# Third layer: keys and values in the second layer's normalisation, queries by halves of the tokens

## The chip, the cores and the metric

One program on one core of a Trainium2 chip. The metric is the device time of one execution in microseconds (us); the kernel before has a median of 1384.41 us in three runs (1384.3 to 1389.26). The engines are TensorE (PE in the rows, with its weight loads as PEld), VectorE (DVE), ScalarE (ACT), GpSimd (POOL) and SyncE (SP), whose queue issues nearly all transfers (DMAs).

## The reference

Four layers follow each other. The first is a large cross-attention with a multilayer perceptron. The second and fourth are alike: 16 heads of 16, keys over the context and the tokens, a root-mean-square normalisation and a perceptron. The third is the one whose start is changed. Cut to what matters:

```python
# 4 batches x 256 tokens, width 256; ctx is an input of the whole program
def layer3(x, ctx, mask):                    # 32 query heads of 8, 8 key/value heads
    q = x @ Wq + bq                          # (4, 256, 256)
    k = ctx @ Wk + bk                        # (4, 256, 64): depends on ctx alone
    v = ctx @ Wv + bv                        # (4, 256, 64): depends on ctx alone
    scores = einsum(q, k) / sqrt(8) + mask   # each key head serves 4 query heads
    out = softmax(scores) @ v @ Wo + bo
    return layernorm(out + x) * gamma + beta
x = layer3(layer2(ctx, layer1(x, ctx), m0), ctx, mask)
x = layer4(ctx, x, m0)
```

## The kernel before

The 1024 tokens (T) lie in 8 tiles of 128 partitions; `core.x` holds them token-major, `core.cT` holds the context feature-major. The program is a row of stages. Each is one block with one instruction stream for each engine, written by hand, and at its end all engines meet; inside, semaphores order them. No scheduler moves anything: the order in the code is the order on each engine, and a DMA is issued when SP reaches it. A stage also ends only when SP has passed its own waits.

The stages around the change, in order:

- `project_out` of the second layer (stage o1) multiplies the attention's output by its matrix and adds the residual.
- `rms_turn` (stage r1) normalises: VectorE takes the statistics of 8 tiles, GpSimd raises them to -1/2, ScalarE scales tiles 0 to 3 and VectorE tiles 4 to 7 (`normed`, L564 and L597). TensorE turns each half with 8 transposes (L611); ScalarE and VectorE split the result into a high and a low part (L568, L601). Beside it the perceptron's first weights are loaded and split, high parts on ScalarE (L1300), low parts on GpSimd (L1305).
- `mlp` (stage m1) is the perceptron; `next_layer` 2 makes SP load the third layer's `wq`, `wkv` and `bv_row` there (L66 to L71).
- `turn` (stage t2) turns `core.x` into `xT`: 16 transposes (L530), and 4 copies on VectorE (L523).
- `wide_projections` (stage p2) computes keys (group 0 and 1, one per half of the tokens), queries (groups 2 to 5: rows `m` 0 with both halves, then `m` 1 with both) and values (8 tiles). For each group TensorE multiplies, VectorE adds the bias (`q_f`), ScalarE rounds it (`q_hi`), VectorE takes the rest (`q_lo`). SP stores keys and queries to DRAM (`k_stack`, `q_stack`) and reads them back in another layout (`load_keys`, `load_queries`). Query stores go by `m`, for all tokens; half of batch 0's heads need only `m` 0, yet SP has `m` 1's stores ahead of their loading:

```python
stores(1)                      # keys
stores(3)                      # queries, m 0, all tokens
sp.wait_ge(k_stored, 16 * 3)
load_keys(c, sp, k_stack, k_st, 0, first_in)
stores(5)                      # queries, m 1, all tokens
sp.wait_ge(q_stored[0], 16 * 3)
load_queries(c, sp, q_stack, q_st, 0, slice(0, c.NQ // 2), first_in)
sp.wait_ge(mask_in, 16); sp.wait_ge(q_stored[1], 16 * 3); sp.wait_ge(first_in, 16 * 8)
```

- `wide_attention` (stage s2) takes 32 quads (4 heads of one batch). Its SP stream first loads the other half of batch 0's queries, then keys and queries of batches 1 to 3. Its first scores are L1887.

The fourth layer (stages p3, s3 and so on) uses `pair_attention`, as the second does; its rounds end with the copy L2023.

Of the kernel before, what the change touches and what calls it, by code (L numbers as in the profile page):

```python
# [5 lines left out]
P = 128  # L6
B = 4
# [499 lines left out]
def turn(core, name, src, xT):  # L507

    nc, ident = core.nc, core.ident
    with core.stage(name) as st:  # L510
        turned = st.psum("turned", [P, 4, 512])
        tile_turned = st.sem("tile_turned")
        chunks = [(kt, slice(half * 512, (half + 1) * 512)) for half in range(2) for kt in range(KT)]
        with nc.Block() as block:
            @block.gpsimd
            def _(pool):
                core.clear_used(pool)

            @block.vector
            def _(dve):  # L520
                for n, (kt, cols) in enumerate(chunks):
                    dve.wait_ge(tile_turned, n + 1)
                    nc.vector.tensor_copy(xT[:, kt, cols], turned[:, n, :])  # L523

            @block.tensor
            def _(pe):
                for half in range(2):
                    for kt in range(KT):
                        for i in range(4):
                            mm = nc.tensor.transpose(turned[:, KT * half + kt, i * P:(i + 1) * P],  # L530
                                                     src[:, 4 * half + i, kt * P:(kt + 1) * P], ident[:])
                        mm.then_inc(tile_turned, 1)


def rms_turn(core, name, src, ahead, eps, scale):
# [6 lines left out]
    with core.stage(name) as st:  # L542
# [9 lines left out]
        chunks = [(kt, slice(half * 512, (half + 1) * 512)) for half in range(2) for kt in range(KT)]  # L552

        with nc.Block() as block:
            @block.sync
            def _(sp):
                ahead.prepare_sync(sp, z)

            @block.scalar
# [1769 lines left out]
```

## Time and profile before

| what | us |
|---|---|
| median of three runs | 1384.41 |
| profiled execution, its own time | 1390.04 |
| its span | 1388.2 |
| PE busy in the span | 1230.7 (89%) |
| last operation of the second layer's perceptron begins | 969.01 |
| first scores of the third layer begin | 1001.86 |
| o1: SP issues its two loads, the second ends | 896.5 |
| o1: its last operation ends, on VectorE | 906.69 |
| `wq` of the second layer: issue to landing, median of 2 | 5.9 |

The profiled execution is 5.6 us longer than the median, near the slowest of the three runs. Times inside it are read from the span's start; 1.84 us lie around the span. A row of the timeline has start, duration, engine, line, operation, out<-in, shapes and count; in brackets stands how long the engine had been idle and what released it. SPq is the issue of a DMA by SP, not its transfer. A matmul of plain f32 shows as two rows' worth of instructions (x8 for 4 matmuls).

### The profile page before, as it was taken

The page shows a single profiled execution, that of the slowest core. Times are in us where ns is not written, and L with a number is a line of the kernel's source. Part 1 is how long each engine was busy: PE and PEld are TensorE (multiplying, and loading weights), DVE is VectorE, ACT ScalarE, POOL GpSimd, SP SyncE. Part 2 cuts the span into 40 slices and gives each one's busy share as a digit, 9 for nine tenths or more (in the row PEclk, how much of TensorE's full clock was granted, in tenths as well). Part 3 has the DMA queues.
Part 4 walks back from the last instruction along what each step waited for, and adds up shares of the span by engine and source line. Part 5 has one row for each costly group of instructions (what it writes and reads, how often), then busy time and mean ns, then how long its engine had stood idle before and what let it go on. Part 6 is the DMA issues. An engine that isn't in the chain of part 4 may idle for free. (4 is left out here: it accounts for less than half of the span.)

```text
span 1388.2 us, 27413 instructions
## 1 busy us (share of the span) xinstructions
PE 1230.7 (89%) x9144; PEld 1014.5 (73%) x9144; DVE 987.8 (71%) x2229; ACT 722.0 (52%) x1636; POOL 495.6 (36%) x642
## 2 busy tenths in 40 slices
PE   5799999999599999999699699969499977699869
PEld 4699999999499999998588455559277756455558
DVE  6478878787578887888763689465488865689464
ACT  4456655666366666566542177441166632177441
POOL 3654545444374445543150000030199940000030
PEclk9899999999799999999899699979799998699979
DMA  4111111010211111010023874020660014874020
GB/s 151 47 31 32 31 30 30 23 30 1 95 32 32 31 31 29 9 38 0 31 65 71 121 83 56 13 77 1 196 131 3 2 51 83 112 81 55 13 65 31
DMA packets 55406, 70.90 MB, mean 51 GB/s; under 512 B 6696, under 2 KB 47404, under 8 KB 52976
## 3 DMA queue, kind: packets, MB, share of 16 engines
q1 hardware_dynamic: 53704, 65.83, 22.8%
q10 hardware_dynamic: 1600, 3.76, 0.9%
q8 instruction: 57, 0.93, 0.3%
q14 instruction: 45, 0.37, 0.1%
HBM read 46.79 MB, written 8.13 MB: 40 GB/s over the span
## 5 line engine op out<-in xcount | busy, mean ns | idle before, releaser
L945 ACT ACTIVATE a_prob<-a_s_ps,a_negmax 128x257 f32<-128x257 f32 x256 | 119.2, 477 | 92.9 <-DVE a_negmax L1027 92.9
L2033 DVE TENSOR_REDUCE s_mx<-s_s_ps 128x2 f32<-128x1024 f32 x128 | 151.9, 1211 | 17.9 <-PE s_s_ps L2078 17.6
L2018 ACT ACTIVATE s_probT<-s_st_ps 128x512 f32<-128x512 f32 x256 | 132.1, 605 | 58.6 <-PE s_st_ps L2092 56.3
L884 POOL TENSOR_TENSOR x_v_hi<-a_v_sum,x_one 128x512 fp32r<-128x512 f32 x60 | 63.2, 1053 | 248.7 <-DVE a_v_sum L1016 248.7
L1822 POOL TENSOR_SCALAR s_below<-s_masked,s_mx 128x256 f32<-128x256 f32 x256 | 117.8, 480 | 30.5 <-DVE s_mx L1850 29.7
L576 POOL TENSOR_TENSOR rstd<-base,power 128x4 f32<-128x4 f32 x4 | 4.0, 1009 | 335.6 <-DVE base L593 335.6
L1042 DVE TENSOR_TENSOR a_pT_lo<-a_t_ps,a_pT_hi 128x512 fp32r<-128x512 f32 x128 | 88.3, 690 | 37.9 <-ACT a_pT_hi L958 36.2
L1027 DVE TENSOR_REDUCE a_negmax<-a_s_ps 128x2 f32<-128x514 f32 x128 | 87.0, 689 | 35.6 <-PE a_s_ps L1088 35.3
L958 ACT ACTIVATE a_pT_hi<-a_t_ps 128x512 fp32r<-128x512 f32 x128 | 76.7, 600 | 59.5 <-PE a_t_ps L1142 56.1
L1850 DVE CUSTOM_DVE_ANT_0 s_masked<-s_s_ps,l_mask 128x256 f32<-128x256 f32 x256 | 90.7, 421 | 16.6 <-PE s_s_ps L1887 16.6
L1835 ACT ACTIVATE s_probT<-s_st_ps 128x512 f32<-128x512 f32 x128 | 69.9, 596 | 29.1 <-PE s_st_ps L1897 29.0
L1086 PE MATMUL a_s_ps<-x_k_hi,x_q_hi 128*128 128x258 f32 x256 | 75.0, 293 | 10.8 <-ACT a_prob L945 5.5
L2078 PE MATMUL s_s_ps<-l_k_st,l_q_st 49*128 49x512 f32 x192 | 68.0, 543 | 15.9 <-PEq L1531 9.5
L1086 PE MATMUL a_o_ps<-a_pT_hi,x_v_hi 128*128 128x256 f32 x256 | 81.1, 317 | 0.0
L1142 PE MATMUL a_t_ps<-ident,a_prob 128*128 128x128 f32 x512 | 78.2, 275 | 3.0 <-ACT a_prob L953 2.0
L2092 PE MATMUL s_st_ps<-l_q_st,l_k_st 50*128 50x256 f32 x384 | 70.4, 339 | 11.0 <-DMA l_q_st<-s_mxT 11.0
L961 ACT ACTIVATE a_oT_hi<-a_o_ps,a_hc 128x256 fp32r<-128x256 f32 x128 | 60.8, 475 | 36.9 <-PE a_o_ps L1088 29.6
L886 POOL TENSOR_TENSOR x_v_lo<-a_v_sum,x_v_hi 128x512 fp32r<-128x512 f32 x60 | 77.3, 1289 | 4.7
L1086 PE MATMUL a_g_ps<-x_wv_hi,c_hi 128*128 128x256 f32 x240 | 70.3, 293 | 7.8 <-POOL x_wv_lo L867 7.8
L2092 PEld LDWEIGHTS s_st_ps<-l_q_st,l_k_st 50*128 50x128 f32 x384 | 48.5, 204 | 34.3 <-DMA l_q_st<-s_mxT 12.8
L1088 PE MATMUL a_s_ps<-x_k_hi,x_q_lo 128*128 128x258 f32 x256 | 72.9, 285 | 0.0
L1087 PE MATMUL a_s_ps<-x_k_lo,x_q_hi 128*128 128x258 f32 x256 | 72.9, 285 | 0.0
(289 smaller groups left out, 4069.0 us busy)
## 6 DMA issues: line engine op xcount, KB each, us to landing
a_wo_raw<-L_xattn_wo SPq DMA_DIRECT2D x16, 256.0 KB, 3.2
x_wqk_raw<-L_xattn_wq SPq DMA_DIRECT2D x31, 128.0 KB, 2.3
x_wqk_raw<-L_xattn_wk SPq DMA_DIRECT2D x31, 128.0 KB, 2.3
x_wv_raw<-L_xattn_wv SPq DMA_DIRECT2D x15, 256.0 KB, 3.0
l_k_st<-k_second SPq DMA_DIRECT2D x12, 256.0 KB, 9.6
l_k_st<-k_stack SPq DMA_DIRECT2D x16, 192.0 KB
l_q_st<-q_stack SPq DMA_DIRECT2D x12, 192.0 KB
x_vbias<-L_xattn_bias_v SPq DMA_DIRECT2D x2, 1024.0 KB, 11.0
```

The costliest lines, as they stand in the source:

```text
L886: nc.gpsimd.tensor_tensor(lo, raw, hi.bitcast(F32), ALU.subtract).then_inc(z.v_split, 1)
L945: nc.scalar.activation(prob[:, n % 2, qt, 0:NK], s_ps[:, n % 2, qt, 0:NK], ACT.Exp, bias=negmax[:, n % 2, qt:qt + 1], accum_out=den[:, n % ...
L958: nc.scalar.activation(pT_hi[:, n % 2], t_ps[:], ACT.Copy).then_inc(z.t_hi, 1)
L1027: nc.vector.tensor_reduce(negmax[:, n % 2], s_ps[:, n % 2, :, 0:NK], AX.X, ALU.max, negate=True).then_inc(z.max_done, 1)
L1042: nc.vector.tensor_tensor(pT_lo[:, n % 2], t_ps[:], pT_hi[:, n % 2].bitcast(F32), ALU.subtract).then_inc(z.t_out, 1)
L1086: nc.tensor.matmul(out, a_hi, b_hi, start=start, stop=False)
L1142: mm = nc.tensor.transpose(t_ps[:, at:at + P], prob[:, n % 2, qt, kt * P:(kt + 1) * P], core.ident[:])
L1822: nc.gpsimd.tensor_scalar(below[:, i % 2, h, qt], masked[:, i % 2, h, qt], -1.0, mx[:, i % 2, h, qt:qt + 1], ALU.mult, ALU.add).then_inc(z ...
L1850: nc.vector.tensor_tensor_reduce(out=masked[:, i % 2, h, qt], in0=s_ps[:, h, qt], in1=mask[:, i // NQ * QT + qt], scale=1.0, scalar=-3.0e3 ...
L2018: nc.scalar.activation(probT[:, third % 2, n // 4, n // 2 % 2, n % 2], st_ps[:, u % 3], ACT.Exp, scale=c.scale).then_inc(z.exp_done, 1)
L2033: nc.vector.tensor_reduce(mx[:, i % 2, qt, a::2], s_ps[:, n % 2], AX.X, ALU.max).then_inc(z.max_done, 1)
L2092: mm = nc.tensor.matmul(st_ps[:, u % 3, j * S:(j + 1) * S], k[:, a, kt * P:(kt + 1) * P], q[:, a], start=True, stop=True)
```

## The change

Three things are done.

1. Keys and values of the third layer are computed in r1, the normalisation of the second layer, by a new class `WideKeys`. SP stores the keys there; the values stay in SBUF (`v_tok`) and GpSimd copies them into `v_st` in p2. For that the third layer's weights are loaded in o1 instead of m1.
2. Stage t2 goes; p2 itself turns `core.x`, the copies shared between VectorE and ScalarE.
3. Queries are computed and stored by halves of the tokens (half 0 holds batches 0 and 1): groups are now (m 0, half 0), (m 1, half 0), (m 0, half 1), (m 1, half 1). SP loads batch 0's keys first, and its queries before the stores of half 1; those are waited for only at batch 2 (`q_late`).

```diff
+class WideKeys:            # k_ps, v_ps: PSUM; f, hi, lo: the keys and their parts, 64 x 1024
+    def keys(self, pe, half):
+        for kt in range(KT):
+            mm = self.nc.tensor.matmul(self.k_ps[0:KW, half], core.wkv[:, kt, 0:KW], core.cT[:, kt, self.cols(half)],
+                                       start=(kt == 0), stop=(kt == KT - 1))
+        mm.then_inc(self.k_done, 1)
+    def values(self, pe):  # 8 tiles x 2 matmuls of 64 columns
...
+    def high(self, act, half):   # two ACTIVATEs: f = k_ps + bias, hi = f
...
+    def low(self, pool, half):   # lo = f - hi
...
+    def store(self, sp):
+        for part, (kept, slots) in enumerate(((self.hi, (0, 2)), (self.lo, (1,)))):
+            sp.wait_ge((self.hi_done, self.lo_done)[part], 2)
+            for n in slots:
+                sp.dma_start(self.front.k_stack[:, n], kept[:].bitcast(F32)).then_inc(self.front.k_stored, 16)
+    def add_bias(self, dve):     # v_tok = v_ps + bias, one 128 x 512 TENSOR_TENSOR
...
 # rms_turn
             def _(act):
+                if keys:
+                    keys.high(act, 0)
                 ahead.prepare_scalar(act, z)
...
+                if keys:
+                    keys.high(act, 1)
                 for n, (kt, cols) in enumerate(chunks):
...
+                if keys:
+                    keys.low(pool, 0)
                 ahead.prepare_pool(pool, z)
+                if keys:
+                    keys.low(pool, 1)
...
+                if keys:
+                    keys.add_bias(dve)
                 for n, (kt, cols) in enumerate(chunks):
...
             def _(pe):
+                if keys:
+                    for half in range(2):
+                        keys.keys(pe, half)
+                    keys.values(pe)
...
 # wide_projections, SP
+                sp.wait_ge(front.k_stored, 3 * 16)
+                load_keys(c, sp, front.k_stack, k_st, 0, z.first_in)
                 sp.dma_start(mask[:], ins["mask_Bx1xSxS2_ff0"].rearrange("b o (t p) k -> p (b o t) k", p=P)
...
+                store(0, z.q_stored0)
+                store(1, z.q_stored1)
+                sp.wait_ge(z.q_stored0, 3 * 16)
+                load_queries(c, sp, front.q_stack, q_st, 0, slice(0, c.NQ // 2), z.first_in)
+                for g in range(2, 4):
+                    store(g, front.q_late)
+                sp.wait_ge(z.mask_in, 16)
+                sp.wait_ge(z.q_stored1, 3 * 16)
+                sp.wait_ge(z.first_in, 16 * 8)
...
 # wide_attention, SP
+                    if b == B // 2:
+                        sp.wait_ge(front.q_late, 6 * 16)
...
 # project_out, SP
                 if next_layer:
-                    core.load_projections(sp, next_layer, next_in)
+                    sp.wait_ge(next_in, core.load_projections(sp, next_layer, next_in))
```

SP's queue in p2 before, from the mask to the last load ahead of the attention (`l_` tiles are in SBUF, `_stack` in DRAM):

```order
L1699 DMA l_mask<-mask_Bx1xSxS_ff 128x8x256
L1683 DMA k_stack<-p_k_hi 8x8x1024 x2
L1683 DMA k_stack<-p_k_lo 8x8x1024
L1687 DMA q_stack<-p_q_hi 16x8x1024 x2
L1687 DMA q_stack<-p_q_lo 16x8x1024
L1640 DMA l_k_st<-k_stack 24x8x256 x4
L1687 DMA q_stack<-p_q_hi 16x8x1024 x2
L1687 DMA q_stack<-p_q_lo 16x8x1024
L1647 DMA l_q_st<-q_stack 24x4x256 x4
L1689 UNCONDITIONAL_BRANCH
```

The same queue and stage of the changed kernel:

```order
L1765 DMA l_mask<-mask_Bx1xSxS_ff 128x8x256
L1759 DMA q_stack<-p_q_hi 16x8x512 x2
L1761 DMA q_stack<-p_q_lo 16x8x512
L1759 DMA q_stack<-p_q_hi 16x8x512 x2
L1761 DMA q_stack<-p_q_lo 16x8x512
L1706 DMA l_q_st<-q_stack 24x4x256 x4
L1759 DMA q_stack<-l_q_hi 16x8x512 x2
L1761 DMA q_stack<-l_q_lo 16x8x512
L1759 DMA q_stack<-l_q_hi 16x8x512 x2
L1761 DMA q_stack<-l_q_lo 16x8x512
L1740 UNCONDITIONAL_BRANCH
```

The four key loads now stand ahead of the mask, the key stores are gone from the stage, query stores are halved in size and doubled in number, and six of them stand behind the four query loads. GpSimd in r1 and m1, before (`w_w_lo` is the perceptron's first weights' low part, `m_w_lo` the second's):

```order
L576 TENSOR_TENSOR rstd<-base,power 128x4 x2
L1305 TENSOR_TENSOR w_w_lo<-w_w_raw,w_w_hi 128x1024 x2
L554 UNCONDITIONAL_BRANCH
L1330 UNCONDITIONAL_BRANCH
L106 ISA x12
L1336 TENSOR_TENSOR m_w_lo<-m_w_raw,m_w_hi 128x512 x4
```

and of the changed kernel:

```order
L625 TENSOR_TENSOR rstd<-base,power 128x4 x2
L560 TENSOR_TENSOR r_k_lo<-r_k_f,r_k_hi 64x512
L1364 TENSOR_TENSOR w_w_lo<-w_w_raw,w_w_hi 128x1024 x2
L560 TENSOR_TENSOR r_k_lo<-r_k_f,r_k_hi 64x512
L597 UNCONDITIONAL_BRANCH
L1389 UNCONDITIONAL_BRANCH
L106 ISA x17
L1395 TENSOR_TENSOR m_w_lo<-m_w_raw,m_w_hi 128x512 x4
```

One subtraction stands ahead of the weights' low parts, one behind. ScalarE in r1, before:

```order
L1300 ACTIVATE w_w_hi<-w_w_raw 128x1024 x2
L564 ACTIVATE r_normed<-a_o_all,rstd 128x256 x4
L568 ACTIVATE w_h_hi<-r_turned,cols 128x512 x4
L554 UNCONDITIONAL_BRANCH
L1385 UNCONDITIONAL_BRANCH
```

and of the changed kernel:

```order
L552 ACTIVATE r_k_f<-r_k_ps,cols 64x512
L555 ACTIVATE r_k_hi<-r_k_f 64x512
L1359 ACTIVATE w_w_hi<-w_w_raw 128x1024 x2
L611 ACTIVATE r_normed<-a_o_all,rstd 128x256 x4
L552 ACTIVATE r_k_f<-r_k_ps,cols 64x512
L555 ACTIVATE r_k_hi<-r_k_f 64x512
L617 ACTIVATE w_h_hi<-r_turned,cols 128x512 x4
```

Two key operations stand ahead of the weights' high parts, two between the scaling and the turned halves.

## Rows read from the trace of the kernel before

**Rows 1.** Timeline of all engines, from the turning of the tokens to the first scores.

```profile
969.76 1.94 PE L530 MATMUL t_turned<-ident,x_tok 128*128 128x128 f32 x16 [0.78 <-PEq L1329]
...
976.76 7.13 PE L1727 MATMUL p_qk_ps<-x_xT,wq 128*128 128x512 f32 x16
...
988.30 0.23 DVE L1762 TENSOR_TENSOR l_v_st<-p_v_ps,bv_row 128x64 f32<-128x64 f32 x1 [0.22 <-PE p_v_ps L1735]
...
1001.86 0.81 PE L1887 MATMUL s_s_ps<-l_k_st,l_q_st 24*128 24x256 f32 x8 [13.60 <-PEq L1689]
```

**Rows 2.** Timeline of SP's queue, 969 to 1060 us.

```profile
985.42 3.82 SPq L1640 DMA_DIRECT2D l_k_st<-k_stack  x4
989.28 1.16 SPq L1687 DMA_DIRECT2D q_stack<-p_q_hi  x2
990.49 2.04 SPq L1687 DMA_DIRECT2D q_stack<-p_q_lo  x1
992.58 10.78 SPq L1647 DMA_DIRECT2D l_q_st<-q_stack  x8
1003.40 1.69 SPq L1640 DMA_DIRECT2D l_k_st<-k_stack  x4
```

**Rows 3.** Windows: stretch, length, busy of each engine, clock, DMA share, GB/s.

```profile
976.00:978.00 2.00, 2.00 (x5) 0.68 (x4) 1.13 (x2) 0.91 (x2) 0.00 (x0) 1.00 0.99 348
...
1012.10:1030.00 17.90, 17.90 (x206) 12.63 (x205) 14.87 (x84) 12.60 (x25) 17.08 (x39) 1.00 0.85 158
```

**Rows 4.** Groups of instructions by shape, 969 to 1002 us.

```profile
L1735 PE MATMUL p_v_ps<-wkv,ctxT 128*128 128x64 f32 x32 | 3.9, 275 | 0.6 <-DVE l_v_st L1762 0.6
...
L1747 DVE TENSOR_SCALAR p_q_f<-p_qk_ps,cols 128x512 f32<-128x512 f32 x4 | 3.0, 750 | 1.7 <-PE p_qk_ps L1727 1.7
...
L1770 ACT ACTIVATE p_q_hi<-p_q_f 128x512 fp32r<-128x512 f32 x4 | 2.5, 631 | 4.5 <-DVE p_q_f L1747 4.5
...
L1751 DVE TENSOR_TENSOR p_q_lo<-p_q_f,p_q_hi 128x512 fp32r<-128x512 f32 x3 | 2.0, 681 | 0.0
```

**Rows 5.** Timeline of the normalisation of the second layer (r1), all engines.

```profile
907.01 1.41 DVE L585 BATCH_NORM_STATS2 stats<-a_o_all 128x6 f32<-128x256 f32 x4 [0.32 <-PEq L2145]
...
910.74 1.06 ACT L1300 ACTIVATE w_w_hi<-w_w_raw 128x1024 fp32r<-128x1024 f32 x1 [16.50 <-DMA w_w_raw<-L_xattn_mlp_w]
...
912.13 4.70 POOL L1305 TENSOR_TENSOR w_w_lo<-w_w_raw,w_w_hi 128x1024 fp32r<-128x1024 f32 x2
...
913.01 1.69 ACT L564 ACTIVATE r_normed<-a_o_all,rstd 128x256 f32<-128x256 f32 x4
...
917.57 1.97 PE L611 MATMUL r_turned<-ident,r_normed 128*128 128x128 f32 x8 [0.84 <-DVE r_normed L597]
...
921.35 0.76 PE L1359 MATMUL m_h_ps<-w_h_hi,w_w_hi 128*128 128x512 f32 x1 [1.81 <-PEq L554]
```

**Rows 6.** Timeline of VectorE in short stretches: the first scaling alone, the last three.

```profile
912.20 2.43 DVE L597 TENSOR_SCALAR r_normed<-a_o_all,rstd 128x256 f32<-128x256 f32 x1 [1.13 <-POOL rstd L576]
...
914.55 2.96 DVE L597 TENSOR_SCALAR r_normed<-a_o_all,rstd 128x256 f32<-128x256 f32 x3
```

**Rows 7.** Windows around the perceptron's start, and at the end of the values.

```profile
926.00:927.00 1.00, 1.00 (x4) 0.76 (x4) 0.00 (x0) 0.16 (x1) 0.00 (x0) 0.59 1.08 345
...
983.00:988.40 5.40, 4.63 (x35) 3.87 (x33) 3.92 (x12) 1.26 (x2) 0.00 (x0) 0.99 0.96 321
988.40:1001.80 13.40, 0.00 (x0) 0.00 (x0) 0.12 (x1) 0.00 (x0) 0.00 (x0) 0.50 0.72 213
```

**Rows 8.** Timeline of the pair attention: ends of rounds, clock full, then half.

```profile
840.16 0.39 ACT L2023 ACTIVATE s_oT<-s_ox_ps 128x256 f32<-128x256 f32 x1 [1.03 <-PE s_ox_ps L2105]
...
846.07 0.39 ACT L2023 ACTIVATE s_oT<-s_ox_ps 128x256 f32<-128x256 f32 x1 [1.05 <-PE s_ox_ps L2105]
...
882.82 0.38 ACT L2023 ACTIVATE s_oT<-s_ox_ps 128x256 f32<-128x256 f32 x1 [2.63 <-PE s_ox_ps L2105]
...
889.86 0.38 ACT L2023 ACTIVATE s_oT<-s_ox_ps 128x256 f32<-128x256 f32 x1 [2.62 <-PE s_ox_ps L2105]
```

More of the change, by code:

```diff
@@ L504, in _ @@
                         queries.products(pe, g)
[L507 to L532, printed above, removed]
@@ new lines, in wide_projections, with cols, whole, high @@
+        heads = front.q_stack.rearrange("g j n d t -> (g j) n d t")
+        groups = [(m, half) for half in range(2) for m in range(KT)]
+        def cols(half):
+            return slice(half * 512, (half + 1) * 512)
+        def whole(g):
+            m, half = groups[g]
+            return q_f[:, m, cols(half)]
+        def high(g):
+            m, half = groups[g]
+            return (q_early, q_late)[half][0][:, m]
+        def low(g):
+            m, half = groups[g]
+            return (q_early, q_late)[half][1][:, m]
@@ L1710, in _, with store @@
-                sp.wait_ge(k_stored, 16 * 3)
-                load_keys(c, sp, k_stack, k_st, 0, first_in)
-                stores(5)
-                sp.wait_ge(q_stored[0], 16 * 3)
-                load_queries(c, sp, q_stack, q_st, 0, slice(0, c.NQ // 2), first_in)
-                sp.wait_ge(mask_in, 16)
-                sp.wait_ge(q_stored[1], 16 * 3)
-                sp.wait_ge(first_in, 16 * 8)
+                def store(g, sem):
+                    m, half = groups[g]
+                    out = heads[P // c.HD * m:P // c.HD * (m + 1), :, :, cols(half)]
+                    sp.wait_ge(z.q_hi, g + 1)
+                    for n in range(2):
+                        sp.dma_start(out[:, n], high(g).bitcast(F32)).then_inc(sem, 16)
+                    sp.wait_ge(z.q_lo, g + 1)
+                    sp.dma_start(out[:, 2], low(g).bitcast(F32)).then_inc(sem, 16)
@@ new lines, in _ @@
+                        mm.then_inc(z.tile_turned, 1)
+                for g, (m, half) in enumerate(groups):
+                    pe.wait_ge(z.x_act, half + 1)
+                    pe.wait_ge(z.x_dve, half + 1)
+                    for kt in range(KT):
+                        mm = nc.tensor.matmul(q_ps[:, g], core.wq[:, kt, m * P:(m + 1) * P], xT[:, kt, cols(half)],
+                                              start=(kt == 0), stop=(kt == KT - 1))
+                    mm.then_inc(z.q_done, 1)
@@ L1767, in _ @@
             def _(act):
+                for half in range(2):
+                    act.wait_ge(z.tile_turned, KT * half + 2)
+                    nc.scalar.activation(xT[:, 1, cols(half)], turned[:, KT * half + 1], ACT.Copy).then_inc(z.x_act, 1)
                 for g in range(len(groups)):
-                    act.wait_ge(qk_f, g + 1)
-                    nc.scalar.activation(places(q_hi, k_hi, g), places(q_f, k_f, g), ACT.Copy).then_inc(qk_hi, 1)
-def wide_attention(core, c, q_stack, k_stack, o_all, q_st, k_st, v_st, mask):
+                    act.wait_ge(z.q_f, g + 1)
+                    nc.scalar.activation(high(g), whole(g), ACT.Copy).then_inc(z.q_hi, 1)
@@ L2261, in small_layer @@
                 mask = st.sb("mask", [P, B * QT, S])
-                with core.stage(f"x{layer}", holds_others=True) as turned:
-                    xT = turned.sb("xT", [P, KT, T])
-                    turn(core, f"t{layer}", core.x, xT)
-                    wide_projections(core, c, xT, q_stack, k_stack, q_st, k_st, v_st, mask)
-                wide_attention(core, c, q_stack, k_stack, o_all, q_st, k_st, v_st, mask)
+                q_late = [st.sb(n, [P, KT, T // 2], F32R) for n in ("q_hi", "q_lo")]
+                wide_projections(core, c, front, q_late, q_st, k_st, v_st, mask)
+                wide_attention(core, c, front, o_all, q_st, k_st, v_st, mask)
             else:
```

187 lines of the change are left out of this document (90 added, 97 removed).

## The prediction

> **What bounds the kernel now.** I first read the timeline of the third layer's start, since the diff changes what stands between the second layer's perceptron and the first scores. Turning begins at 969.76, the last arithmetic of the stage ends at 988.53, and the first scores stand at 1001.86: 32.1 us, of which the last 13.3 have no engine at work [rows 1]. The row of the scores names only the stage's end as their releaser, so the reason has to be read from the queue of SP. There the four key loads are issued from 985.42, the stores of the second half of the queries' rows at 989.28 and 990.49, and the query loads only from 992.58 [rows 2]. The windows say what the transfers do meanwhile: 213 GB/s on average while all engines are idle [rows 7], 348 GB/s while only the mask moves, and 158 GB/s while loads of 1 KB rows from the stacks move [rows 3]. So this stage is bound by transfers and by their order on SP, not by its 19 us of arithmetic.
>
> The second place is the normalisation r1, which receives work. Its end is set by VectorE's four scalings: the first lasts 2.43 us, from 912.20, the other three together 2.96, so that two of them take about 0.3 each if the second is like the first [rows 6]; GpSimd's two subtractions run from 912.13 to 916.83 [rows 5]. Two scalings end 0.1 us after a GpSimd operation each, and only then the other two are short. After 917.51 the second half's turning, splitting and the stage change lead to the perceptron's first matmul at 921.35 [rows 5].
>
> **The third layer's start, part by part.** Removed from p2: the keys' 8 and the values' 32 matmul instructions, about 3.6 and 3.9 us of TensorE, a whole stage change, 768 KB of key stores. What is left:
>
> - TensorE turns from 969.76 to 971.70 [rows 1]. The two engines that share the copies follow it closely, so queries start at about 971.8. A group is 7.13/4 = 1.78 us [rows 1]; results stand at about 973.8, 975.6, 977.3 and 979.1.
> - One group's chain is now strictly serial on VectorE: 0.75 bias, 0.63 high part, 0.68 low part [rows 4] and some 0.2 of handing over, 2.26 us. High parts are ready at 975.2, 977.5, 979.7, 982.0, low parts at 976.0, 978.3, 980.6, 982.8. Arithmetic ends at 982.8 instead of 988.5.
> - GpSimd's two memsets and eight copies of 128x64 have until the attention. No row has such a copy. A 128x1024 subtraction is 2.35 us (4.70/2) [rows 5], by columns 0.15 for 64; even at five times that, eight cost 6 us and end 10 us before the attention. GpSimd has nothing else there: zero.
> - SP: key loads take 0.42 us each unpressed (1.69/4), 0.96 pressed (3.82/4) [rows 2], and end by 971.4 to 973.6. The first half's six query stores follow their parts, the last about 979 to 980.5. The four query loads wait until the first group's stores have landed, about 981.3, and cost about 2 us. Behind them stand six more stores before SP may end the stage; a store costs 0.58 (1.16/2) or, pressed, 2.04 [rows 2]. I take 0.9, nearer the first, as half a store's data presses less: 983.3 + 5.4 = 988.7.
> - The transfers themselves: loads of 768 + 384 KB at 158 GB/s are 7.5 us, mask and first stores 1024 + 1536 KB at 348 GB/s another 7.5 [rows 3]. Begun at 971, back to back, they end at 986.0, and with landing and stage change (about 1 us) the scores cannot start before 987.0.
>
> SP's path is the later one: 988.8 with the branch. Gain 1001.86 - 988.8 = 13.1 us, bounds 14.9 (the transfers' floor) and 6.2 (six stores at 2.04 us end at 995.5, so 995.7). After the start nothing is late: the other half of batch 0's queries is queued behind 1.5 MB of stores, 4.5 us at 348 GB/s, and is wanted only at the fifth quad; `q_late` is wanted at the seventeenth.
>
> **The normalisation r1.** TensorE is idle there from 907 on until the first turning, which waits for ScalarE's scaling to 914.70 [rows 5]. Keys and values need 3.6 + 3.9 = 7.5 us at full clock [rows 1, 4], from about 907.1 to 914.6: hidden, by 0.1 us. ScalarE's first two key operations (0.63 each, as L1770) end near 910.5, before the weights' at 910.74 [rows 5]: hidden. Its second two push the first half's splitting by about 0.2 us; that is not the late side.
>
> The late side is VectorE. GpSimd gets a 64x512 subtraction ahead of the weights and one behind; by columns half of 4.70/2, thus 1.2 us each [rows 5]. If a scaling again gets through only at the end of a GpSimd operation, the four ends are 913.3, 915.7, 918.0 and 919.2, and the fourth scaling ends at 919.3 instead of 917.5: +1.8. The values' bias (128x512, about 0.7 us) then runs while the second half is being turned; +0.1. If the fourth slips in before the last subtraction it is +0.9; without any queueing 0. If instead the values run at half clock, twice 3.9 us, turning begins at 918.5, the second half's 1.97 us after it [rows 5], so +2.9. I take +1.9, the ordering that rows 6 show.
>
> The perceptron starts at half clock and gets the full one at about 926.6: the window 926 to 927 has 0.59 [rows 7]. From 921.35 that is 5.2 us, 2.6 lost. If the rise does not move with the start, a start 1.9 us later loses 0.9 less; if it moves, nothing. I take 0.5 back. SP's key stores wait for the last low part at about 919.2 and take less than 1 us: done before the stage's end at 922.9.
>
> The weights' load moves to o1, behind the two transfers needed there, and adds a wait at o1's end, 907.0 [rows 5]. No row shows that wait. Its last load is issued at about 898.3, and even the slowest single landing that the page lists for such a load, in the small table, is 5.9 us. Zero; if it were late, its price would be what it exceeds 907.0 by, at most 1 or 2 us. m1 loses four loads that nothing waited for: zero.
>
> Sum: -13.1 + 1.9 - 0.5 = -11.7 us. Against the profiled execution, 1390.04 - 11.7 = 1378.3. That execution was 5.6 us above the median; I carry the difference to the median: 1384.41 - 11.7 = 1372.7 us.
>
> **Rivals.** (A) SP's queue becomes the bound: with the queue full, the six late stores cost up to 2.04 us each and hold the stage's end, though no engine needs them. For it: 2.04 for one store, 3.82 for four loads [rows 2]. Against: at 1.16 for two the same stores were cheap, and the first half's data are gone by then. Scores at 995.7: -6.2 + 1.4 = -4.8, 1379.6 us.
>
> (B) TensorE's clock stays at 2.4 GHz through r1, since its idle gap is filled. Then the perceptron loses none of its 2.6 us and the second turning shrinks from 1.97 to about 1: 3.6 less instead of my 0.5, so 1369.6 us. Against it: in 983 to 988.4 TensorE was busy 4.63 of 5.40 us, mostly with just these values, and the clock was 0.50 from 988.4 on [rows 7].
>
> The Trainium skill (TensorE: Matmul & The Clock Gate, "Part 1: The HAM clock gate") has the clock follow how busy TensorE has lately been, which taken plainly is case B; the trace agrees only in part, as the fall right behind 4.63 busy us shows.
>
> (C) Slower: the fourth layer's attention runs its rounds at half clock. A round is 5.91 us at full clock (846.07 - 840.16) and 7.04 at half (889.86 - 882.82) [rows 8], 1.13 more. The 13 us shift moves every later wait against the clock's changes. If all 16 rounds stay low it costs 18.1 us, 1390.8 us; it outweighs the gain from 11 rounds on. For it: the clock does fall within that attention's twin. Against: it recovered there each time, and the code after the change is the same.
>
> (D) The gain is as forecast but more executions land in the upper of the times seen (1389.26 against 1384.3), which is +5: 1377.7 us.
>
> **How the numbers follow.** Forecast 0.70, A 0.10, B 0.10, C 0.03, D 0.07. The range must reach B with the transfers' floor (1369.6 - 1.8 = 1367.8) and, on the other side, A at 1379.6 or D with a little less gain; 1367 to 1380 leaves out C and tails, about 0.1. 0.5% of the median is 6.9 us, about what a measurement of this kernel can tell from no change: the bound is 1377.5. Faster holds the forecast with nearly all its spread, B, and a part of A and D: 0.68 + 0.10 + 0.03 + 0.03 = 0.84. Slower by over 0.5% (above 1391.3) holds half of C and the unforeseen: 0.03. The rest, 0.13, is within.
>
> **What would show it.** Scores of the third layer 19 to 20 us after its turning begins (32.1 now); 17.5 would mean the transfers' floor, 26 case A, with SP's last stores late. In r1, four scalings with three of them over 1 us and an end about 7.1 us after the first began (5.3 now). The clock at the perceptron's first matmul still 0.50; 1.00 there is B. In the fourth layer the same span for its attention, or C. I am wrong if the scores still wait 10 us with no engine at work, or if r1 grows by more than 3 us.

## The result, and the profile after

The changed kernel has a median of 1375.65 us in nine runs (1369.83 to 1377.44), beside 1384.3 us for the kernel before in nine (1379.56 to 1389.26): ratio 0.9933, 95% interval 0.9911 to 0.9954. Two more comparisons gave 0.9942 (0.9920 to 0.9964) and 0.9927 (0.9904 to 0.9949). By these ratios the change is worth 8 to 10 us; the medians lie 8.65, 6.9 and 7.1 us apart. The forecast was 11.7 us less and a median of 1372.7 us, in a range of 1367 to 1380.

Executions of one and the same kernel lie some 10 us apart (1379.56 to 1389.26 before), and the two profiled ones (1390.04 before, 1369.83 after) happen to be a long one and a short one: 20 us between them, half of it not from the change. So I compare not whole spans but the three stretches that the change touches, each from an event to an event of one trace, and over all the profiles there are: two of the kernel before, three of the changed one.

| stretch, us | before | changed | difference of means |
|---|---|---|---|
| r1: first statistics to the perceptron's first matmul | 14.34, 14.36 | 16.80, 16.79, 16.79 | +2.4 |
| m1: from there to the turning of the tokens | 48.41, 48.67 | 47.55, 48.73, 47.40 | -0.6 |
| p2: from the turning to the first scores | 32.10, 31.41 | 19.87, 19.94, 20.28 | -11.7 |
| all three | 94.85, 94.44 | 84.22, 85.46, 84.47 | -9.9 |

9.9 us less lies within what the ratios say (0.9933 of 1384 is 9.3 less) and is more than the medians lie apart. Inside a stretch the traces of one kernel repeat within 0.7 us, r1 within 0.02; m1 of the changed kernel alone spreads by 1.3, by the clock (below). The -0.6 of m1 is not shown to come from the change: two traces of an experiment whose r1 and m1 are those of the kernel before ("The order alone") have 47.20 and 47.34 there. Without it the change is -9.3.

In its profiled execution the changed kernel has a span of 1368.0 us, with TensorE busy for 1220.3 (1230.7 before) on the same 9144 matmul instructions.

**The third layer's start.** Timeline of the changed kernel, all engines, turning to first scores, which answers to [rows 1]:

```profile
969.64 1.94 PE L1782 MATMUL p_turned<-ident,x_tok 128*128 128x128 f32 x16 [0.78 <-PEq L1388]
...
971.42 7.11 PE L1789 MATMUL p_q_ps<-p_xT,wq 128*128 128x512 f32 x16
...
972.85 1.48 POOL L1749 COPY l_v_st<-parts_v_tok 128x64 f32<-128x64 f32 x8
...
989.51 0.81 PE L1932 MATMUL s_s_ps<-l_k_st,l_q_st 24*128 24x256 f32 x8 [10.98 <-PEq L1740]
```

The arithmetic ends at 981.7 (VectorE's last low part begins at 981.01) instead of 988.5, the scores come 19.9 us behind the turning instead of 32.1, and TensorE still stands idle for 11 us ahead of them. The eight copies of the values by GpSimd take 0.19 us each, far from the late side. SP's queue in the same stretch, which answers to [rows 2]:

```profile
969.59 1.63 SPq L1699 DMA_DIRECT2D l_k_st<-k_stack  x4
...
978.12 0.60 SPq L1761 DMA_DIRECT2D q_stack<-p_q_lo  x1
982.98 1.55 SPq L1706 DMA_DIRECT2D l_q_st<-q_stack  x4
984.57 1.17 SPq L1759 DMA_DIRECT2D q_stack<-l_q_hi  x2
...
987.89 0.93 SPq L1761 DMA_DIRECT2D q_stack<-l_q_lo  x1
989.46 2.02 SPq L1706 DMA_DIRECT2D l_q_st<-q_stack  x4
```

and its waits (engine, line, what it waited for; total, count, longest):

```profile
SPq L1706 <- DMA q_stack<-p_q_lo: 4.2, 1, 4.2
```

SP waits 4.2 us, from 978.72, until the stores of the first group (`m` 0, half 0) have landed; the loads go out in 1.55 us, and the six stores behind them pass in 4.25 us, 0.7 each. No wait for a landing follows them: the stage ends and SP's next load is issued 0.6 us after the last of them (987.89 + 0.93 to 989.46). What the transfers do meanwhile (stretch, its length, busy of each engine, clock, DMA share, GB/s), beside [rows 7] with 213 GB/s:

```profile
969.60:982.00 12.40, 8.89 (x32) 4.69 (x32) 6.89 (x10) 3.71 (x6) 3.37 (x10) 1.00 0.92 223
982.00:989.50 7.50, 0.00 (x0) 0.02 (x1) 0.00 (x0) 0.03 (x1) 0.00 (x0) 0.62 0.89 278
```

The DMA engines are nearly full from the turning on (share 0.92 and 0.89; it was 0.72 in the idle stretch before). No engine is at work for the last 7.8 us (981.7 to 989.5), 13.3 before.

**The normalisation r1.** Timeline of all engines, which answers to [rows 5]:

```profile
905.29 1.41 DVE L638 BATCH_NORM_STATS2 stats<-a_o_all 128x6 f32<-128x256 f32 x4 [0.32 <-PEq L2190]
905.29 3.62 PE L537 MATMUL r_k_ps<-ctxT,wkv 128*64 128x512 f32 x8 [0.78 <-PEq L2190]
...
908.84 3.79 PE L545 MATMUL r_v_ps<-wkv,ctxT 128*128 128x64 f32 x32
...
909.84 1.06 ACT L1359 ACTIVATE w_w_hi<-w_w_raw 128x1024 fp32r<-128x1024 f32 x1 [1.27 <-DMA w_w_raw<-L_xattn_mlp_w]
...
910.42 1.27 POOL L560 TENSOR_TENSOR r_k_lo<-r_k_f,r_k_hi 64x512 fp32r<-64x512 f32 x1
...
911.65 4.67 POOL L1364 TENSOR_TENSOR w_w_lo<-w_w_raw,w_w_hi 128x1024 fp32r<-128x1024 f32 x2
...
916.28 1.30 POOL L560 TENSOR_TENSOR r_k_lo<-r_k_f,r_k_hi 64x512 fp32r<-64x512 f32 x1
...
918.31 1.97 PE L670 MATMUL r_turned<-ident,r_normed 128*128 128x128 f32 x8 [3.37 <-DVE r_normed L650]
...
922.09 0.77 PE L1418 MATMUL m_h_ps<-w_h_hi,w_w_hi 128*128 128x512 f32 x1 [1.81 <-PEq L597]
```

and VectorE's scalings in short stretches, which answer to [rows 6]:

```profile
910.48 5.98 DVE L650 TENSOR_SCALAR r_normed<-a_o_all,rstd 128x256 f32<-128x256 f32 x1 [1.12 <-POOL rstd L625]
...
916.39 1.35 DVE L650 TENSOR_SCALAR r_normed<-a_o_all,rstd 128x256 f32<-128x256 f32 x1
...
917.65 0.60 DVE L650 TENSOR_SCALAR r_normed<-a_o_all,rstd 128x256 f32<-128x256 f32 x2
```

Keys and values run at full clock and end at 912.63, before the first turning: hidden. The first scaling takes 5.98 us, from the start of GpSimd's run of four operations to the end of its third; the second gets through at the end of the fourth; the last two take 0.3 each. Windows around the perceptron's start (columns as above):

```profile
915.00:925.00 10.00, 4.87 (x15) 3.95 (x16) 6.68 (x9) 3.84 (x6) 2.58 (x2) 0.52 0.39 124
925.00:926.00 1.00, 1.00 (x4) 0.77 (x4) 0.25 (x1) 0.69 (x1) 0.00 (x0) 0.65 1.07 381
926.00:927.00 1.00, 1.00 (x6) 0.82 (x5) 0.18 (x1) 0.20 (x1) 0.00 (x0) 1.00 0.99 331
```

The clock is at its lower level, 1.2 GHz, when the perceptron begins at 922.09, although TensorE had been busy with keys and values from 905.3 to 912.6, and is full from some 3.6 us after that start. In the other two profiles of this kernel the rise came 6.1 and 3.3 us after it, in the two of the kernel before 5.5 and 6.0; the m1 of 48.73 us in the table is the one with 6.1. With the order alone changed, where r1 and m1 are those of the kernel before, it came after 3.0 and 3.2, which is why m1 is 47.20 and 47.34 there.

### The profile page after: what moved, and what is told of

Its sections match the earlier page's. It is cut to its first block and busy times, and to the rows that moved or that the text cites. A ratio compares the mean times of both kernels' runs of the same rounds, so it can differ in the third digit from the quotient of the medians.

```text
span 1368.0 us, 27416 instructions
## 1 busy us (share of the span) xinstructions
PE 1220.3 (89%) x9144; PEld 1008.8 (74%) x9144; DVE 984.4 (72%) x2216; ACT 724.0 (53%) x1640; POOL 501.0 (37%) x652
## 5 line engine op out<-in xcount | busy, mean ns | idle before, releaser
L1867 POOL TENSOR_SCALAR s_below<-s_masked,s_mx 128x256 f32<-128x256 f32 x256 | 118.3, 486 | 17.6 <-DVE s_mx L1895 17.5
L625 POOL TENSOR_TENSOR rstd<-base,power 128x4 f32<-128x4 f32 x4 | 4.0, 1010 | 328.5 <-DVE base L646 328.5
L1147 PE MATMUL a_g_ps<-a_wo_hi,a_oT_lo 128*128 128x256 f32 x256 | 72.7, 284 | 0.0
```

The costliest lines, as they stand in the source:

```text
L1147: return nc.tensor.matmul(out, a_lo, b_hi, start=False, stop=stop)
L1867: nc.gpsimd.tensor_scalar(below[:, i % 2, h, qt], masked[:, i % 2, h, qt], -1.0, mx[:, i % 2, h, qt:qt + 1], ALU.mult, ALU.add).then_inc(z ...
```

## The experiments

The changed kernel and the one before were run again with each group; medians are given with their number of executions, and the ratio is to the kernel before on the same chip.

**The changed kernel again.**

> The changed kernel once more, beside the kernel before on one chip. If the gain is what the third layer's start lost (12.2 us between turning and first scores in the first pair of traces) less what r1 gained (2.5 us longer, of which the clock gave 0.9 back), the medians lie 10 to 11 us apart. If something behind the attention gives part of it back, they lie 6 to 8 apart though the same stretches are as short.

Measured: 1375.89 us (7), before 1382.78 (24), ratio 0.9942 (0.9920 to 0.9964). The medians lie 6.9 apart, not 10 to 11, though the stretches are as short; with this spread that does not show that something behind gives part back. Its trace is the second of the changed kernel in the table: the stretch lasts 85.46 us.

**The kernel before, one more profile.**

> The kernel before, profiled once more. The first pair of traces gave 94.85 us from r1's beginning to the third layer's first scores before and 84.22 after, 10.6 less, while the medians lie 6.9 to 8.7 apart. Theory that these stretches are steady: 94 to 95.5 again, and the missing 2 to 4 us are lost or blurred elsewhere. Rival (the kernel before itself varies there, and its first trace was a long one): 90 to 93 us.

Measured: 1385.12 us in the one execution. Its stretch is 94.44 us beside 94.85: steady, as the theory said. The first trace of before, on which the prediction's sum was made, had its scores 0.7 us later behind the turning than this one.

**GpSimd's low parts of the keys behind the weights' (L625 and following).**

```diff
-                if keys:
-                    keys.low(pool, 0)
                 ahead.prepare_pool(pool, z)
                 if keys:
+                    keys.low(pool, 0)
                     keys.low(pool, 1)
```

> One edit to the changed kernel: GpSimd takes both of the keys' low parts behind the weights' low parts. Theory of the queueing (VectorE's scalings wait for GpSimd's run of operations): one or two of the four scalings finish before the weights begin, the rest at their end, so the scalings end some 2.3 us sooner, r1 lasts 14.4 to 14.8 us instead of 16.8, and the time falls by 1.5 to 2.5 us. Rival (r1 is longer by the added work on TensorE and ScalarE): r1 stays 16.8 and the time the same.

Measured: 1376.51 us (6), ratio 0.9946 (0.9925 to 0.9967), the changed kernel's within the error; the 1.5 to 2.5 us that were expected of the whole time are not seen. Timelines of its r1, GpSimd, then VectorE in short windows:

```profile
913.53 4.72 POOL L1363 TENSOR_TENSOR w_w_lo<-w_w_raw,w_w_hi 128x1024 fp32r<-128x1024 f32 x2 [0.56 <-ACT w_w_hi L1358]
...
918.21 2.55 POOL L560 TENSOR_TENSOR r_k_lo<-r_k_f,r_k_hi 64x512 fp32r<-64x512 f32 x2
```

```profile
913.00 5.40 DVE L649 TENSOR_SCALAR r_normed<-a_o_all,rstd 128x256 f32<-128x256 f32 x4 [1.13 <-POOL rstd L625]
...
913.53 4.87 DVE L649 TENSOR_SCALAR r_normed<-a_o_all,rstd 128x256 f32<-128x256 f32 x2
...
915.96 2.44 DVE L649 TENSOR_SCALAR r_normed<-a_o_all,rstd 128x256 f32<-128x256 f32 x1
```

Two scalings are done before GpSimd begins, in 0.53 us, thus 0.27 each alone; the third begins with GpSimd's first subtraction at 913.53 and ends with it, the fourth ends 0.1 us after the second. The scalings end 10.59 us after the first statistics (12.96 in the changed kernel, 10.50 before) and r1 lasts 14.43: all of the +2.4, to 0.1, comes from where GpSimd's first low part stands. But m1 is 48.56, 0.7 longer than the changed kernel's mean, since the clock rises later after the perceptron's first matmul at 922.24 (5.9 us). The window of the changed kernel's 926 to 927 had 1.00; here:

```profile
927.00:928.00 1.00, 1.00 (x4) 0.74 (x3) 0.00 (x0) 0.27 (x1) 0.00 (x0) 0.50 0.54 176
```

That is still the lower level 5.8 us behind the first matmul. All three profiles with the low parts last have m1 at 48.5 to 48.6, so 0.7 of the 2.4 is given back there. Net, r1 and m1 last 63.0 us instead of 64.7. What happens is that the rise stays where it was: counted from r1's first statistics it comes at 20.1 to 20.6 us in nine of the ten profiles of the changed kernel and its edits (22.9 in the tenth), whether the perceptron begins at 16.8, 16.15, 15.4 or 14.4. A start 2.4 us earlier thus only adds 2.4 us at the lower clock; against the four traces with r1 at 16.8 and the rise in that place (m1 47.4 to 47.6) 1.0 us is given back.

**The first low part between GpSimd's two powers.** VectorE's scalings then begin after it.

```diff
                 for half in range(2):
                     pool.wait_ge(base_done, half + 1)
                     nc.gpsimd.tensor_tensor(out=half_of(rstd, half), ...)
+                    if keys and half == 0:
+                        keys.low(pool, 0)
-                if keys:
-                    keys.low(pool, 0)
                 ahead.prepare_pool(pool, z)
```

> The changed kernel with the first low part of the keys on GpSimd between its two powers, thus before VectorE's first scaling instead of beside it; the second low part stays last. The second power ends some 0.4 us later, and GpSimd's work behind it is the weights' two subtractions and one low part. Theory (the first scaling, which begins beside the first low part, passes over the ends of two GpSimd operations because they follow without a gap, and passes only at the third): with the low part gone from there one scaling gets through at the end of each weights' subtraction, as in the kernel before; the fourth scaling ends about 11.3 us after the statistics begin instead of 12.96, and m1's first matmul is at about 15.2 instead of 16.8. Rival (what counts is the sum of GpSimd's operations from the second power on to the last low part): that sum falls by 1.27 and rises by 0.4, so the end is at about 12.1 and m1 at 15.9. In the median either is within 1.5 us of the changed kernel, 1375.7: 1374 to 1376 us.

Measured: 1372.73 us (7), before 1382.95 (12), ratio 0.9933 (0.9910 to 0.9956). The scalings end at 12.31 and the perceptron starts at 16.15: the rival's 12.1 and 15.9, not the theory's. The median is 1.3 us under the expected 1374 to 1376, the ratio that of the changed kernel. Timelines of its r1, GpSimd, then VectorE:

```profile
906.13 1.26 POOL L560 TENSOR_TENSOR r_k_lo<-r_k_f,r_k_hi 64x512 fp32r<-64x512 f32 x1 [0.20 <-ACT r_k_hi L555]
...
908.85 4.81 POOL L1364 TENSOR_TENSOR w_w_lo<-w_w_raw,w_w_hi 128x1024 fp32r<-128x1024 f32 x2
913.62 1.31 POOL L560 TENSOR_TENSOR r_k_lo<-r_k_f,r_k_hi 64x512 fp32r<-64x512 f32 x1
```

```profile
906.48 0.94 DVE L644 TENSOR_TENSOR r_msq<-mv 128x4 f32<-128x4 f32 x1
...
908.73 6.35 DVE L650 TENSOR_SCALAR r_normed<-a_o_all,rstd 128x256 f32<-128x256 f32 x4 [1.12 <-POOL rstd L625]
...
909.00 2.45 DVE L650 TENSOR_SCALAR r_normed<-a_o_all,rstd 128x256 f32<-128x256 f32 x1
...
911.37 2.44 DVE L650 TENSOR_SCALAR r_normed<-a_o_all,rstd 128x256 f32<-128x256 f32 x1
...
913.73 1.35 DVE L650 TENSOR_SCALAR r_normed<-a_o_all,rstd 128x256 f32<-128x256 f32 x1
```

Here the order is plain: one scaling free (0.27), then one at the end of each of GpSimd's three operations, the last at 915.08. So my theory had the order right and the count wrong, since the fourth still has GpSimd's last low part ahead of it. VectorE's small product L644 shows the same wait: 0.94 us beside GpSimd's low part, 0.16 in the changed kernel.

The Trainium skill (SBUF — State Buffer, "Who interferes with whom") says that GpSimd and some VectorE instructions share a pair of ports as an exclusive lock for a whole instruction, `tensor_scalar` in a two-port mode among them, and that whoever comes first blocks the other. The trace agrees with the blocking (0.27 us alone, 2.4 beside one GpSimd subtraction). Why a waiting scaling in the changed kernel is passed by two GpSimd instructions in a row (ends at 911.7 and 914.0, before the first gets through at 916.4) is open.

**The old order of SP's queue in the changed kernel**: second half's stores ahead of the query loads.

```diff
-                sp.wait_ge(z.q_stored0, 3 * 16)
-                load_queries(c, sp, front.q_stack, q_st, 0, slice(0, c.NQ // 2), z.first_in)
                 for g in range(2, 4):
                     store(g, front.q_late)
+                sp.wait_ge(z.q_stored0, 3 * 16)
+                load_queries(c, sp, front.q_stack, q_st, 0, slice(0, c.NQ // 2), z.first_in)
...
+                sp.wait_ge(front.q_late, 6 * 16)
```

> The changed kernel with the old order on SP in the third layer's start: all twelve query stores ahead of batch 0's query loads, and all of them waited for at the stage's end. Theory of the order: the loads queue behind 1.5 MB more of stores, so turning to scores takes 22 to 24 us instead of 19.9 and the time rises by 2 to 4 us. Rival (the gain is the keys' and values' removal alone, the order is worth nothing): 19.9 us and the same time.

Measured: 1378.75 us (12), ratio 0.9972 (0.9957 to 0.9987), 2.9 above the changed kernel of the same group. Its p2 lasts 21.90, 1.9 more, just under the 22 to 24 that the theory had. SP's queue there, and its waits at the stage's end:

```profile
980.58 0.66 SPq L1761 DMA_DIRECT2D q_stack<-l_q_lo  x1
981.37 9.97 SPq L1706 DMA_DIRECT2D l_q_st<-q_stack  x8
```

```profile
SPq L1775 <- DMA q_stack<-l_q_lo: 3.4, 1, 3.4
...
SPq L1776 <- DMA l_q_st<-q_stack: 2.1, 1, 2.1
```

The edit changes two things, the order and a wait for the late stores; that wait (L1775) ends 2.1 us before the landing of the loads (L1776), which ends the stage, so it is the order that costs. By halves all stores are issued by 981.2, just before the loads, and the order is worth 1.9 us. Its r1 lasted only 15.37, with the same instructions there: the weights' DMA landed later, GpSimd paused for 0.23 us behind the low part, the first scaling got through at the low part's end and the second in that gap. GpSimd, then VectorE:

```profile
909.43 1.27 POOL L560 TENSOR_TENSOR r_k_lo<-r_k_f,r_k_hi 64x512 fp32r<-64x512 f32 x1
910.94 4.76 POOL L1364 TENSOR_TENSOR w_w_lo<-w_w_raw,w_w_hi 128x1024 fp32r<-128x1024 f32 x2 [0.23 <-ACT w_w_hi L1359]
```

```profile
909.50 6.34 DVE L650 TENSOR_SCALAR r_normed<-a_o_all,rstd 128x256 f32<-128x256 f32 x4 [1.13 <-POOL rstd L625]
...
911.04 2.45 DVE L650 TENSOR_SCALAR r_normed<-a_o_all,rstd 128x256 f32<-128x256 f32 x1
```

The third scaling begins at 911.04; two were through by then, where in the changed kernel not one was until 916.4.

**The order alone, on the kernel before**: there the stores of `m` 1 go behind the loading of batch 0's first queries, and are waited for at the attention's start (their tiles are kept until then).

```diff
 stores(3)
 ...
-stores(5)
 sp.wait_ge(q_stored[0], 16 * 3)
 load_queries(c, sp, q_stack, q_st, 0, slice(0, c.NQ // 2), first_in)
-sp.wait_ge(q_stored[1], 16 * 3)
+stores(5)
 # wide_attention, SP
+sp.wait_ge(core.late_stored, 16 * 3)
```

> The kernel before with the order alone changed: batch 0's first query loads ahead of the stores of the queries' second half of rows, and those waited for only in the attention. Keys and values stay where they were. Theory of the order: turning to scores falls from 32.1 to 26 to 28 us, the time by 4 to 6 us. Rival (the order is worth nothing while the key stores and loads stand in the queue): 31 to 32 us, the same time.

Measured: 1382.35 us (12), before 1382.78, ratio 0.9994 (0.9979 to 1.0009): the 4 to 6 us that were expected are not there. Yet its trace had the scores 28.39 us behind the turning (993.50 - 965.11), where the kernel before has 32.10 and 31.41. So it ran again. The 27.7 us in the expectation, and with them its 4.5, are counted from 965.80, inside the turning and not from its start:

> The kernel before with its stores behind the query loads, once more. Its trace had the first scores 4.5 us earlier (27.7 us behind the start of turning instead of 32.1 and 31.4), its median moved by 0.4 us. Theory: the gain is real and lay inside the spread of the executions: now 2 to 5 us under the kernel before. Rival: the one trace was a lucky one, most executions have their scores as late as before: within 1 us, and the trace shows 30 us or more.

Measured: 1380.47 us (12), before 1383.83 (17), ratio 0.9974 (0.9963 to 0.9986); scores at 27.67. SP's queue, then the turning and the first scores from TensorE's timeline, and the turning of the run ahead of it:

```profile
985.34 1.55 SPq L1647 DMA_DIRECT2D l_q_st<-q_stack  x4
986.93 1.16 SPq L1687 DMA_DIRECT2D q_stack<-l_q_hi  x2
```

```profile
964.43 1.94 PE L530 MATMUL t_turned<-ident,x_tok 128*128 128x128 f32 x16 [0.78 <-PEq L1329]
...
992.10 0.81 PE L1887 MATMUL s_s_ps<-l_k_st,l_q_st 24*128 24x256 f32 x8 [9.17 <-PEq L1689]
```

```profile
965.11 1.94 PE L530 MATMUL t_turned<-ident,x_tok 128*128 128x128 f32 x16 [0.78 <-PEq L1329]
```

The earlier start is real (3.7 us, mean of two against two), and so is a gain, since the second measurement's interval leaves out no change; but over both the median moved by 0.4 and 3.4 us, about 2. Where the other 2 us go I can't show: the attention, from the first scores to the beginning of ScalarE's last operation, lasts 124.8 and 125.3 us in the two traces, beside 125.3 and 124.3 before. It stays open.

The order is thus worth 3.7 us of the 11.7 when it is put into the kernel before, and 1.9 when it is taken out of the changed one. The other 8.0 to 9.8 us in p2 come from the keys and values, the stage change and the stores by halves together; no run parts these. The rows show one piece: the queries' first matmul stood 7.0 us behind the turning's start before (976.76 - 969.76 [rows 1]) and stands 1.8 behind it now, 5.2 less. Against the whole stand the 1.8 that r1 and m1 pay in the table.

**The second half's stores in the attention stage**, behind its first four loads; the stage p2 then ends on the loads.

```diff
 # wide_projections, SP
-                for g in range(2, 4):
-                    store(g, front.q_late)
 # wide_attention, SP, behind the second load of batch 0's queries
+                for m in range(KT):
+                    out = heads[P // c.HD * m:P // c.HD * (m + 1), :, :, 512:1024]
+                    for n in range(3):
+                        sp.dma_start(out[:, n], front.late[n // 2][:, m].bitcast(F32)).then_inc(front.q_late, 16)
```

> One edit to the changed kernel: the six stores of the queries of half 1 are issued in the attention's stage, behind the second query loads, so SP can end the third layer's start right after batch 0's query loads. Theory (SP's queue is the later path, the transfers' floor lies 1.8 us below): turning to scores falls from 19.9 to 17 to 18.5 us, the time by 1.5 to 2.5. Rival (the landing of the query loads ends the stage in both): 19.5 to 20 us, no change.

Measured: 1374.24 us (10), before 1383.98 (21), ratio 0.9940 (0.9920 to 0.9960). First scores at 18.27; the 1.5 to 2.5 us that were expected of the whole time are not seen, the ratio is that of the changed kernel. SP's loads and its wait at the stage's end, and TensorE:

```profile
982.79 6.36 SPq L1706 DMA_DIRECT2D l_q_st<-q_stack  x8
```

```profile
SPq L1773 <- DMA l_q_st<-q_stack: 2.8, 1, 2.8
```

```profile
987.66 0.81 PE L1935 MATMUL s_s_ps<-l_k_st,l_q_st 24*128 24x256 f32 x8 [9.38 <-PEq L1740]
```

The stage's start gains 1.8 us of the 2.5 that stood above the 17.5 which the prediction gave as the transfers' floor. So the six stores did hold the stage's end. They take 4.25 us of SP's queue, but without them the landing of the loads holds it, 2.8 us behind their issue, and so they cost 1.8. At 0.7 each they are nearer the sum's 0.9 than case A's 2.04.

**Filling TensorE's gap ahead of the scores**: 12 matmuls of f32 without use behind the queries, to keep the clock up.

```diff
+                for n in range(12):
+                    nc.tensor.matmul(turned[:, n % 4], core.wq[:, 0, 0:P], xT[:, 0, cols(0)], start=True, stop=True)
```

> One edit to the changed kernel: TensorE does twelve more matmuls of 512 columns (about 10 us) into a PSUM tile that nothing reads any more, in the gap between the queries and the first scores, to hold its clock. Theory (the attention's first 8 us at half clock cost 2 to 4 us): the clock is 1.00 at the first scores, the attention's stretch falls from 124.5 to 121 to 123 us. Rival (its start waits for VectorE and GpSimd): 124 us as now, no change of time.

Measured: 1376.28 us (12), ratio 0.9950 (0.9934 to 0.9967), no better than the changed kernel. The added matmuls run from 979.39 for 10.5 us. TensorE's first scores and the window around them (0.50 in that stretch of the changed kernel):

```profile
990.21 0.51 PE L1934 MATMUL s_s_ps<-l_k_st,l_q_st 24*128 24x256 f32 x8 [0.36 <-PEq L1740]
```

```profile
990.00:997.40 7.40, 4.77 (x40) 3.92 (x40) 5.60 (x32) 3.40 (x5) 5.76 (x13) 0.83 0.80 207
```

The first eight scores take 0.51 instead of 0.81 us, the mean clock is 0.83 instead of 0.50, and the attention lasts 123.6 us, beside 124.3, 124.8 and 124.0. That is under a microsecond, not the 2 to 4 of the theory, and nothing that the median can tell. In the window TensorE is busy 4.77 of 7.40 us and VectorE 5.60: the half clock is not what the attention's start waits for most.

**Both edits together**, the low parts last and the stores in the attention.

> Both edits together on the changed kernel: the keys' low parts behind the weights', and half 1's stores in the attention's stage. If both act on stretches that follow each other, r1 is 14.4 and turning to scores 17 to 18.5 us, and the time falls by 3 to 5 us against the changed kernel. If their gain is taken back later it falls by less than 2, as with the low parts alone (r1 shorter by 2.4 us, the medians 0.6 apart).

Measured: 1369.73 us (6), ratio 0.9904 (0.9882 to 0.9926). Then again, and beside it the changed kernel:

> The changed kernel with both edits (GpSimd's two low parts of the keys behind the weights' subtractions; the second half's stores behind the loads that the first scores need), once more, beside the changed kernel on the same chip. Theory: the two edits take 2.4 us out of the normalisation and 1.5 us out of the third layer's start; the perceptron gives 1 back, so it stands 3 us below the changed kernel, about 1372 to 1373 us. Rival: the earlier median of 1369.7 us came from only six executions, and what the edits win is lost in the attention's start; then the two kernels stand within 1 us of each other.

> The changed kernel beside the one with both edits. Both theories: about 1375.7 us, 8 us under the kernel before; its stretch from the statistics to the first scores 84 to 86 us in its trace.

Measured: both edits 1373.42 us (6), ratio 0.9912 (0.9886 to 0.9938); the changed kernel 1376.75 us (6), ratio 0.9927 (0.9904 to 0.9949), its stretch 84.47. The stretch of both edits from the statistics to the scores lasts 81.37 and 80.88 us, 3.6 less than the changed kernel's mean of 84.7, and in the second comparison its median stands 3.3 lower, as the theory had it; six executions each don't part the two for certain. It is the best version that was run: 12 to 13 us under the kernel before by its ratios.

## Why the prediction was right, and what of it was off

**The bound was read rightly.** The stage waited for its transfers and for their order on SP. Both halves of the remedy are seen: the order alone brought the scores 3.7 us forward, the rest 8.0.

**The third layer's start: forecast -13.1, measured -12.2 between the two first traces and -11.7 over all.** The forecast put the scores 19.0 us behind the turning (988.8 - 969.76), the traces have 19.9, 19.9 and 20.3. Of the steps: queries from 971.8 (971.42 measured, from a turning 0.1 earlier); arithmetic to the end by 982.8 (981.7); GpSimd's copies at no cost (they end at 974.3). The step that failed is "the first group's stores have landed, about 981.3": SP waited until 982.98, 1.7 more. Most of it was made good by what follows: the loads took 1.6 instead of 2 and the late stores 4.25 instead of 5.4, 0.7 us each instead of 0.9. The stage change then took 0.7 (988.82 to 989.51) where the sum had 0.1. So 19.0 against 19.9 is closer than its terms are. The remaining 0.5 between -12.2 and -11.7 is mostly the trace of before, longer by 0.7 at this place than the second one. One sum of the prediction is off: its floor is written as 17.5, but 987.0 - 969.76 is 17.2. The weights' loading in o1 cost nothing, as said: r1's first operation stands 0.32 us behind o1's last in both kernels.

**The normalisation: forecast +1.9, measured +2.4.** VectorE was the late side, as said, and hidden work was hidden. The ordering was not as said. I let one scaling through at the end of each GpSimd operation, four of them, and the fourth ends at 12.3 us after the statistics (919.3 - 907.01). In the changed kernel the first scaling was passed over twice; one got through at the end of the third operation, one at the end of the fourth, and the last two came behind, which makes 12.97. The run of scalings lasts 7.8 us (910.48 to 918.26) with two of them over 1 us, where the prediction's sign was 7.1 with three. Here the scalings end when GpSimd's run ends, plus what is left of them at 0.3 each. That is the latest they end, and no rule: with the low parts last they end 2.4 us before GpSimd's run does, and with a pause in it 1.1 before. With the first low part between the powers one got through at the end of each operation, as I had it, but behind a free first one; that the end is 12.31, the prediction's 12.3, is luck, since another sequence gives it.

**The clock: forecast -0.5, measured -0.6 in m1.** It was at half at the perceptron's start in spite of 7.4 busy microseconds before, so B's gain did not come. Keys and values themselves ran at full clock; behind them TensorE turns for 1.09 us and then waits from 914.9 to 918.3 for VectorE's scalings, and the clock is at half when it goes on. The agreement in size is luck. The forecast took the middle of two cases, and the measured figure is a mean of two: -1.1 where the rise came 3.3 to 3.6 us after the perceptron's start, +0.2 where it came 6.1 after. And over all four traces with the r1 and m1 of the kernel before, m1 is 47.9, the changed kernel's mean too.

**The rivals.** A: the late stores did hold the stage's end, but took 0.7 each, not 2.04, and cost 1.8 in all. C: in the fourth layer the clock was at half for 30.7 us (1174.9 to 1205.6), as long as before (1189.7 to 1220.4), and the rounds behind it follow each other every 5.9 us. Only two near the end differ: 7.3 and 6.9, 7.1 and 7.3 us in two of the changed kernel's traces and 5.7 and 5.4 in the third, 7.1 and 7.3 in the first trace of before and 5.7 and 6.5 in its second. That is part of the spread of both kernels, not the 16 rounds of C. D: no more executions in the upper times (1369.83 to 1377.44). The median of nine is 2.95 us above the forecast, of which the sum's own error explains 1.8 (11.7 - 9.9), or 2.4 if m1's 0.6 is not counted, and the rest lies within the intervals.

## What to carry to other kernels

Where a stage ends with all engines idle, read the issue queue first: a store that nobody needs yet, ahead of a load that somebody waits for, costs its landing and not just its issue. Work that is hidden on its own engine can still be paid for by another: ask of each GpSimd instruction that is added which VectorE instructions stand beside it, and put it behind them. And when single executions differ by more than the effect, compare the stretches that the change touches, in several traces, before believing a median or a span.

## What the runs showed of the hardware that was not expected

- A VectorE scaling of 128x256 f32 takes 0.27 us alone and up to 5.98 us beside a run of GpSimd subtractions. It gets through at the end of each GpSimd instruction in the kernel before and in three of the edited ones (low parts last, one between the powers, old order), but in the changed kernel and two other edits it is passed over at two ends and gets through at the third (five profiles, all alike). With a pause of 0.23 us behind the first GpSimd instruction the first gets through at that instruction's end and the second in the pause. What decides between these was not found.
- In the same code the clock rose at different times after the perceptron's first matmul (three profiles of the changed kernel: 3.6, 6.1, 3.3; the r1 and m1 of the kernel before: 5.5, 6.0, 3.0, 3.2), and that is worth 1.2 us. Where r1 was shortened the rise did not come along (low parts last: 5.9, 5.7, 5.7; old order, r1 at 15.4: 5.2; one low part between the powers, r1 at 16.15: 4.2), so a microsecond gained ahead of it was worth little more than half of one (2.4 gained in r1, 1.0 lost in m1).
- SP's stores of 256 KB by halves took 0.5 to 0.9 us each to issue with DMA share near 0.9 in the changed kernel's first trace, and 1.4 once in another, where a store of the whole had taken up to 2.04 [rows 2].
